# Counting 53,125 arcs per node with 64 x 50 digits instead of 128 x 25, and two small products that restore the layout

## The reference

```python
h = x
for l in range(3):
    msg  = concat(h[src], h[dst]) @ Mw.T + Mb          # one row per arc
    deg  = segment_sum(1, dst)                         # arcs per node
    s1, s2 = segment_sum(msg, dst), segment_sum(msg*msg, dst)
    mx, mn = segment_max(msg, dst), segment_min(msg, dst)
    ...                                                # std, var, degree scalers, update,
    ...                                                # batch norm over nodes, mix, layer norm, elu
out = layernorm(x + h)
```

## Time and profile before

| | |
|---|---|
| median of 3 runs | 1983.93 us (1983.11 to 1986.06) |
| the profiled execution, its own time | 1980.07 us |
| its span, first to last instruction | 1978.4 us |
| busy: POOL, PE, DVE, ACT | 69%, 66%, 37%, 15% |
| chain that ended last, by line | POOL's gathers of line 509 56%; issue 19% |
| histogram's first one-hots start | 10.15 us |
| first gather of line 453 starts | 55.38 us |
| first gather of a layer (line 509) starts | 133.66 us |

### The profile page before, as it was taken

The page is one execution under the profiler, slowest core; times in us unless marked ns, Lnnn a source line. Parts: engine busy times, 40 slices in busy tenths (PEclk is TensorE's granted clock), DMA queues, the critical chain, the costliest instruction groups (busy, mean ns, idle before and its releaser), DMA issues.

```text
span 1978.4 us, 15330 instructions
## 1 busy us (share of the span) xinstructions
PE 1299.7 (66%) x4667; PEld 897.7 (45%) x4667; DVE 740.6 (37%) x1751; ACT 288.5 (15%) x656; POOL 1368.9 (69%) x1414
## 2 busy tenths in 40 slices
PE   6626767766666556776767666674777776666663
PEld 5425545544444334554445444433555454444431
DVE  8823433333333242333333332242433333333336
ACT  0124100000000152101010000044111010000023
POOL 2657777777777456777777777717777777777725
PEclk9967998788888787888887788786998888888776
DMA  6253333333333213333333333313333333333310
GB/s 67 73 142 103 102 101 102 101 102 102 101 101 101 78 66 91 101 104 102 101 102 102 102 101 102 101 38 98 103 102 104 102 103 102 101 102 102 101 32 33
DMA packets 85323, 186.68 MB, mean 94 GB/s; under 512 B 32644, under 2 KB 41943, under 8 KB 85231
## 3 DMA queue, kind: packets, MB, share of 16 engines
q0 software_dynamic: 64816, 173.72, 29.9%
q1 hardware_dynamic: 20420, 11.94, 3.2%
HBM read 172.00 MB, written 14.96 MB: 95 GB/s over the span
## 4 chain that ended last, share of the span: by engine, by line
POOL 57%; issue 19%; PE 6%; DMA 4%; DVE 4%; ACT 2%; POOLq 1%; DVEq 0%; ACTq 0%
POOL G L509 56%; DMA G<-p_table,index 4%; PE ps L636 3%; PE ps L689 1%; PE ps L659 1%; DVE hT L1227 1%; POOL p_table L472 1%; PE ps L696 1%; POOLq L507 1%; POOL rows_by_rank L463 1%; ACT G L843 1%; ACT G L840 1%; DVE hT L1229 0%; PE ps L698 0%; DVE acc L1047 0%
## 5 line engine op out<-in xcount | busy, mean ns | idle before, releaser
L509 POOL DMA_INDIRECT G<-p_table,index x1242 | 1226.5, 987 | 398.5 <-issue 388.4
L636 PE MATMUL ps<-G,ident 128*128 128x256 f32 x2484 | 786.4, 470 | 473.3 <-DMA G<-p_table,index 472.3
L636 PEld LDWEIGHTS ps<-G,ident 128*128 128x128 f32 x2484 | 551.4, 233 | 686.8 <-DMA G<-p_table,index 593.9
L1047 DVE TENSOR_TENSOR acc<-G 128x512 f32<-128x512 f32 x150 | 97.0, 689 | 516.2 <-DMA G<-p_table,index 503.3
L1058 DVE TENSOR_TENSOR acc<-acc,G 128x512 f32<-128x512 f32 x132 | 91.5, 693 | 427.3 <-DMA G<-p_table,index 427.3
L659 PE MATMUL ps<-w_u_sb,aggT 128*128 128x384 f32 x600 | 209.5, 493 | 0.0
L659 PEld LDWEIGHTS ps<-w_u_sb,aggT 128*128 128x128 f32 x600 | 115.8, 194 | 82.9 <-ACT aggT L785 5.1
L472 POOL DMA_INDIRECT p_table<-base,index x50 | 52.0, 1039 | 94.4 <-issue 93.2
L797 ACT ACTIVATE uT<-ps,v_sb 128x128 f32<-128x128 f32 x75 | 27.6, 367 | 502.3 <-PE ps L666 502.3
L1059 DVE TENSOR_TENSOR acc<-acc,G 128x512 f32<-128x512 f32 x132 | 90.4, 685 | 0.0
L785 ACT ACTIVATE aggT<-ps 128x512 f32<-128x512 f32 x75 | 44.8, 597 | 239.1 <-PE ps L646 239.1
(11 more groups left out here) (179 smaller groups left out, 1014.7 us busy)
## 6 DMA issues: line engine op xcount, KB each, us to landing
G<-p_table,index POOLq DMA_INDIRECT x1242, 2.8
p_table<-G SPq DMA_DIRECT2D x6, 512.0 KB, 3.0
w_u_sb<-in_w_u SPq DMA_DIRECT2D x3, 768.0 KB, 4.0
x_r<-rows_by_rank SPq DMA_DIRECT2D x1, 1600.0 KB, 9.9
windows<-src_pad SPq DMA_DIRECT2D x1, 1118.0 KB, 22.7
p_table<-base,index POOLq DMA_INDIRECT x50, 2.4
index<-rows_by_rank SPq DMA_DIRECT2D x1, 487.5 KB, 4.7
base<-windows,row_i POOLq DMA_INDIRECT x25, 2.5
```

The source lines that it names most:

```text
L509: g.indirect_dma_start(G[:, n % R, j, :, :].rearrange("p a d -> p (a d)"), None, p_table, bass.IndirectOffsetOnAxis(ap=index[:, t, k0 + j: ...
L636: ins = mm(out_ps, ident[:, :], G[:, n % R, k, :, :].rearrange("p a d -> p (a d)"), start=False, stop=n in END and k == nk - 1)
L1047: ins = TT(acc[:, i, :, :], first, here, op)
```

## The change

The low digit has 64 values (`& 63`) and the high one 50 (`>> 6`). The iota table, `hot_lo` and the weights of a product have 64 columns in place of 128; `hot_hi` and the streamed slice have 50 in place of 25. The counts come out as 64 x 50. They are copied to `count_sb`; two products with shifted identity matrices (`spread`, 64 x 192, made by POOL with one memset and one affine select) put even columns on partitions 0 to 63 and odd ones on 64 to 127, and a second copy takes the 128 x 25 result to `deg`, as before.

```diff
--- before.py
+++ after.py
@@ -84,6 +84,8 @@
     BATCHES = [(0, 7), (7, 13), (13, 19), (19, T)]
     SP_LEN = STRIDE * (NW - 1) + WL
     BINS = 64
+    LO = 64
+    HI = -(-NP // LO)
     BB = BINS // 4
     GW = 4
     GROUPS = []
@@ -179,8 +181,10 @@
         place = carve(2 * BINS * T).rearrange("p (a f) -> p a f", a=2)
         win_f = carve(2 * T * WL).rearrange("p (a f) -> p a f", a=2)
         win_i = carve(T * WL).bitcast(I32).rearrange("p (t k) -> p t k", k=WL)
-        digits = carve(P * HC // 2).bitcast(BF16).rearrange("p (j c) -> p j c", c=HC)
+        digits = carve(LO * HC // 2).bitcast(BF16).rearrange("p (j c) -> p j c", c=HC)
         hot_bin = carve(BINS * T // 2).bitcast(BF16).rearrange("p (b t) -> p b t", t=T)
+        spread = carve(LO + P)[0:LO, :]
+        count_sb = carve(HI)[0:LO, :]
         slot_no = carve(T * KW).rearrange("p (t k) -> p t k", k=KW)
         ones_f = carve(P)
         before_f = carve(P)
@@ -188,8 +192,8 @@
         before_b = carve(P // 2).bitcast(BF16)
 
         carve = carver(G_flat, R * GW * 2 * D)
-        hot_lo = carve(P * HC)[0:EP, :].bitcast(BF16).rearrange("p (b j c) -> p b j c", b=2, c=HC)
-        hot_hi = carve(T * HC)[0:EP, :].bitcast(BF16).rearrange("p (b j c) -> p b j c", b=2, c=HC)
+        hot_lo = carve(LO * HC)[0:EP, :].bitcast(BF16).rearrange("p (b j c) -> p b j c", b=2, c=HC)
+        hot_hi = carve(HI * HC)[0:EP, :].bitcast(BF16).rearrange("p (b j c) -> p b j c", b=2, c=HC)
         dst_i = carve(EC)[0:EP, :].bitcast(I32)
         digit_i = carve(2 * EC)[0:EP, :].bitcast(I32).rearrange("p (b c) -> p b c", b=2)
         digit_b = carve(EC)[0:EP, :].bitcast(BF16).rearrange("p (b c) -> p b c", b=2)
@@ -250,6 +254,7 @@
         s_digits = sem("digit_hots")
         s_hist = sem("digit_hots_used")
         s_cnt = sem("degrees_counted")
+        s_spread = sem("degrees_spread")
         s_deg = sem("degrees_copied")
         s_pre = sem("degree_prefixes")
         s_bins = sem("bin_hots")
@@ -420,12 +425,13 @@
             g = nc.gpsimd
             g.memset(zeros_i[:, :], 0).then_inc(s_const, 1)
             g.memset(rows[:, T - 1, 0:D], 0.0).then_inc(s_xpad, 1)
-            g.iota(digits[:, :, :], [[1, P], [0, HC]], base=0, channel_multiplier=0,
+            g.iota(digits[:, :, :], [[1, LO], [0, HC]], base=0, channel_multiplier=0,
                    allow_small_or_imprecise_dtypes=True).then_inc(s_const, 1)
             g.memset(ones_b[:, :], 1.0)
             g.memset(ones_f[:, :], 1.0)
             g.memset(ones_d[:, :], 1.0 / D)
             g.memset(ident[:, :], 0.0)
+            g.memset(spread[:, :], 0.0)
             g.memset(centre[:, :], -1.0 / D)
             g.memset(eps_ln[:, :], LN_EPS)
             g.memset(eps_std[:, :], STD_EPS)
@@ -439,6 +445,8 @@
             g.affine_select(out=ident[:, :], in_=ident[:, :], compare_op=ALU.not_equal, fill=1.0,
                             base=0, pattern=[[-1, P]], channel_multiplier=1)
 
+            g.affine_select(out=spread[:, :], in_=spread[:, :], compare_op=ALU.not_equal, fill=1.0,
+                            base=LO, pattern=[[-1, LO + P]], channel_multiplier=1)
             g.affine_select(out=centre[:, :], in_=centre[:, :], compare_op=ALU.not_equal, fill=1.0 - 1.0 / D,
                             base=0, pattern=[[-1, P]], channel_multiplier=1)
             g.affine_select(out=before_f[:, :], in_=ones_f[:, :], compare_op=ALU.is_gt, fill=0.0,
@@ -531,7 +539,7 @@
         @block.tensor
         def _(pe):
             mm = nc.tensor.matmul
-            cnt = ps[:, 0, 0:T]
+            cnt = ps[0:LO, 0, 0:HI]
 
             def count(b, first, last):
                 for c in range(HC):
@@ -552,6 +560,10 @@
             count(0, False, True).then_inc(s_hist, 1)
 
             pe.wait_ge(s_const, 4)
+            pe.wait_ge(s_cnt, 1)
+            by_half = count_sb[:, :].rearrange("p (t a) -> p a t", a=2)
+            mm(ps[:, 2, 0:T], spread[:, LO:LO + P], by_half[:, 0, :], start=True, stop=False)
+            mm(ps[:, 2, 0:T], spread[:, 0:P], by_half[:, 1, :], start=False, stop=True).then_inc(s_spread, 1)
             pe.wait_ge(s_deg, 1)
             mm(ps[:, 1, 0:T], before_f[:, :], deg[:, :], start=True, stop=True)
             mm(ps[:, 1, 32:32 + T], ones_f[:, :], deg[:, :], start=True, stop=True).then_inc(s_pre, 1)
@@ -868,8 +880,8 @@
             TT, TS, STT = v.tensor_tensor, v.tensor_scalar, v.scalar_tensor_tensor
 
             dve.wait_ge(s_dst, 16)
-            ch.step(TS(digit_i[:, 0, :], dst_i[:, :], P - 1, None, ALU.bitwise_and))
-            ch.step(TS(digit_i[:, 1, :], dst_i[:, :], 7, None, ALU.logical_shift_right))
+            ch.step(TS(digit_i[:, 0, :], dst_i[:, :], LO - 1, None, ALU.bitwise_and))
+            ch.step(TS(digit_i[:, 1, :], dst_i[:, :], 6, None, ALU.logical_shift_right))
             ch.wait()
             ch.step(v.tensor_copy(digit_b[:, :, :], digit_i[:, :, :]))
             ch.wait()
@@ -879,8 +891,8 @@
             def hots(b, at):
                 lo = digit_b[:, 0:1, bass.ds(at, HC)]
                 hi = digit_b[:, 1:2, bass.ds(at, HC)]
-                TT(hot_lo[:, b, :, :], digits[0:EP, :, :], lo.to_broadcast([EP, P, HC]), ALU.is_equal)
-                TT(hot_hi[:, b, :, :], digits[0:EP, 0:T, :], hi.to_broadcast([EP, T, HC]),
+                TT(hot_lo[:, b, :, :], digits[0:EP, :, :], lo.to_broadcast([EP, LO, HC]), ALU.is_equal)
+                TT(hot_hi[:, b, :, :], digits[0:EP, 0:HI, :], hi.to_broadcast([EP, HI, HC]),
                    ALU.is_equal).then_inc(s_digits, 1)
 
             hots(0, 0)
@@ -893,7 +905,9 @@
             dve.wait_ge(s_hist, HCH - 2)
             hots(0, (HCH - 1) * HC)
             dve.wait_ge(s_hist, HCH)
-            v.tensor_copy(deg[:, :], ps[:, 0, 0:T]).then_inc(s_deg, 1)
+            v.tensor_copy(count_sb[:, :], ps[0:LO, 0, 0:HI]).then_inc(s_cnt, 1)
+            dve.wait_ge(s_spread, 1)
+            v.tensor_copy(deg[:, :], ps[:, 2, 0:T]).then_inc(s_deg, 1)
             dve.wait_ge(s_deg, 1)
 
             ch.step(STT(key_b[:, :], deg[:, :], float(BINS - 2), real[:, :], ALU.min, ALU.add))
```

## The result

The changed kernel takes 2003.38 us (2003.18 to 2003.9) against 1983.52 us (1982.44 to 1986.06) for the kernel before in the same series: ratio 1.0098, 95% interval 1.0085 to 1.0111, so 17 to 22 us slower. I had forecast 5.5 us faster, with 0.07 for slower. The profiled execution took 2003.21 us with a span of 2001.5.

A forecast was written before the change was run, and what follows sets the result against it. The histogram, paced by DVE, was taken to hold up row_i, the gathers and the layers. Start and loop gain 7.03 us, minus 1.48 added, is 5.55: from 1983.93 to 1978.4 us, range 1973.5 to 1983.0.

The forecast's parts named there:

- What bounds the kernel: Whole kernel: one serial string, so time the histogram gives back reaches row_i, the 50 transfers and the three layers.
- The start: Before the histogram: a shorter POOL iota, 2.55 us, lets DVE's first one-hots begin at 8.11 us, 2.04 earlier.
- The one-hots: DVE in the histogram: 1.02 and 0.83 us per chunk, advancing by 1.69 us instead of 2.21.
- What is added: After the histogram: wider first copy, two f32 products and DVE's release add 1.48 us, bounds 1.3 and 1.7.
- The products: PE in the histogram: 64 weight columns and 50 streamed stay at 67.7 ns each, 1.87 us per chunk.
- bound of 95 ns: Histogram product on PE: upper bound if load, 53 ns, and stream, 42 ns, run in series.
- The pace: Histogram chunks: two buffers tie DVE and PE together, giving 1.935 us per chunk.
- the ring: DVE and PE over two histogram buffers: one-hots 1.77, to PE 0.06, products 1.87, return 0.17; 3.87 us for two chunks.
- way back: From PE's last product of a chunk to DVE's next one-hots: 0.17 us, from 0.1 to 0.3.
- The rival of the other side: Histogram products with load and stream in series, PE setting the pace: 1987.7 us at 95 ns, 1997 at 117; chance 0.10.
- formula 12.0 + 424x: End of the histogram's last product in us if PE sets the pace at x per product; gain gone from 86 ns.
- the main case: Histogram paced by the ring as worked out: kernel 1978.4 us, own range 1976.5 to 1980.5; chance 0.55.

The follow-up runs named there:

- the last two kernels: Changed kernel with one-hots in five groups of five columns, weights zero-padded to 128: 1978.95 us, ratio 0.9982; the second also with a 64 x 5 iota first: 1978.34, 0.9975.
- the table: Kernel before plus ten bursts of 40 unused products, differing in weight and stream columns, stepped by 25 or packed: 1989.81 us against 1980.63.
- the grouped kernel without padding: Changed kernel with both one-hots in five groups of five columns, slices stepping by 5 elements, still 64 weight columns: ratio to before 0.9998.
- the wide stream: Kernel before with a high digit one-hot of 50 values, the upper 25 never matching, weights still 128 columns: 1983.31 us against 1980.63.
- The bursts of different steps: Kernel before plus twenty bursts of 24 unused products, with weight or streamed columns stepping by 1 to 48 elements: 2001.72 us against 1976.92.

## Why the prediction was wrong

**What bounds the kernel** held. The delay of the first window gather (18.33 us) was found again at the first layer gather (18.61) and in the median (19.9). The gains of the last two kernels (5.07 and 6.18) arrive at the layers too (4.75 and 6.13), and the medians (3.9 and 4.5) agree with them within their intervals.

**The start** held: iota 2.47 us (2.55 forecast), first one-hots at 8.00 us (8.11). The digit split that had taken 3.26 us beside the long iota took 0.70 once the shorter iota had ended (3.75 us), which fits the picture that DVE was held up beside POOL. **The one-hots** held: 1.04 and 0.84 us. **What is added** held: 1.41 us (1.48).

**The products** is the step that failed. It left a pair at 67.7 ns with 117 as the farthest bound; it measured 134, so a chunk's products take 3.35 us where the prediction had 1.87. Two errors lie in it. I priced a weight column and a streamed one from rows in which the columns lie side by side, 0.82 and 0.84 ns, although every slice of the histogram steps by 25 elements; the table gives 2.1 and 1.8 to 1.9 for such a step. And I took the 67.7 ns of before for something that would stay, without asking what it was. It was the load of 128 stepped columns, four times cheaper per column than a narrow one; with 64 columns this falls away, and half the columns take twice the time. I had cited the rule that says so and gave it the packed price, so its bound of 95 ns was too low. My picture that load and stream overlap was right; in series the two would be about 134 + 92 = 226 ns, an estimate from the table.

**The pace** followed the products, not the ring: PE without a gap, 3.3 us per chunk. The ring itself was reckoned rightly and did not apply. Where it does, in the grouped kernel without padding, its terms give the measured 4.32 us for two chunks, with a way back of 0.16 us (0.17 forecast); with the wide stream they give 2.64 + 0.05 + 2.54 + 0.16 = 5.39, as measured (18.46 to 23.85).

The rival of the other side had the right engine but not the right reason: PE sets the pace because one of the two, the load, has become long, not because load and stream add up. It had a chance of 0.10, and its farthest price of 117 ns was too low. With x = 134 ns its formula 12.0 + 424x gives 68.8 us for the last product, where 66.99 was measured: it has a gap of 0.1 us per chunk that was not there. That it then gives 2004 us for the kernel, where 2003.4 was measured, is in part luck, since the median moved 1.3 us more than the layers' start did.

**The range** of the main case, 1976.5 to 1980.5, is wider than the two terms that it names allow: the way back enters eight times, so 0.1 to 0.3 us of it and 1.3 to 1.7 added give 1977.6 to 1979.6. This plays no part in the miss.

## What to carry to other kernels

The cost of a short product is that of its slower read, weights or stream, and depends on how the columns lie: here 0.83 to 0.94 ns per bf16 column, streamed or of a narrow load, up to a step of 8 bytes, 1.2 at 10 bytes and 1.7 to 2.5 from 16 bytes on, all at TensorE's pace of 1.2 GHz (no run has a stepped product at 2.4). Before the weights are made narrower than 128 columns, ask what the fast load of 128 was worth; zeros up to 128 gave back 40 ns of the 134, and the smaller step 57 of them without any padding. A price from a row with the same operation and type is not a price for the same access pattern, and a pace that no priced row explains deserves a row of its own before it is carried over.

## What the runs showed of the hardware

- A weight load of 64 bf16 columns at a step of 50 bytes takes twice as long as one of 128 (134 against 66.5 ns), one of 96 three times (197).
- Products with 64 stepped weight columns advance at 67 ns when they go to alternate halves of the array, at 134 when to the same half. That the loads overlap is my reading.
- One-hots in five groups with inner runs of 5 elements cost DVE 0.11 and 0.14 us more than with runs of 25, for 1250 and 1600 elements. The grouped layout has one dimension more, which no run separates from the run's length.
- The profile gives the granted clock of the kernel before as 1.00 up to 96 us, but in this stretch the figure does not tell the level. The pair of 128 and 25 stepped columns takes 67 ns in the histogram and 66.5 in the burst where it reads 0.50. And one line of before shows both paces under a reading of 1.00 (timeline of PE, 85 to 96 us; the granted clock reads 1.00 from 90 to 92 and from 94.1 to 95.2):

```profile
90.05 2.08 PE L586 MATMUL ps<-w_p_sb,uT 128*128 128x128 f32 x8
...
94.14 1.16 PE L586 MATMUL ps<-w_p_sb,uT 128*128 128x128 f32 x8
```

Eight products of the same form take 2.05 us in the table's run at 144.06, where the clock reads 0.50, the 1.2 GHz level, and 1.06 at 151.24, where it reads 1.00. By its pace the first stretch ran at 1.2 GHz. The bursts of different steps read 1.00 up to the stream at step 8 and 0.50 at the last ones, with packed columns at 0.83 to 0.85 ns there and 0.83 to 0.87 in the table.
